# State scan of a four-part network: softplus in one activation, convolution sums in SBUF, earlier norm statistics

## The reference, cut to what matters

```python
xz = x @ in_proj_w + in_proj_b
xc, z = jnp.split(xz, 2, axis=-1)
xc = silu(depthwise_causal_conv4(xc) + conv_b)
dBu = xc @ x_proj_w + x_proj_b
delta_s, B, u = jnp.split(dBu, [d_state, 2 * d_state], axis=-1)
delta = jax.nn.softplus(delta_s @ dt_proj_w + dt_proj_b)
A = -jnp.arange(1, d_state + 1)
deltaA = jnp.exp(delta[..., None] * A)
deltaB_u = delta[..., None] * B[:, :, None, :] * u[..., None]
h = dA * h + dBu_      # over time, y = h.sum(-1)
y = (y + u * D) * jax.nn.silu(z)
return y @ out_proj_w + out_proj_b
```

## Time and profile before

| | us |
|---|---|
| median of 3 runs (1362.57 to 1373.91) | 1366.16 |
| the profiled execution | 1378.29 |
| its span in the trace | 1376.6 |
| PE / DVE / ACT / POOL busy in the span | 1197.3 / 904.7 / 782.9 / 291.6 |
| scan: first scan instruction to the end of the last | 1017.40 to 1228.10 |

### The profile page before, as it was taken

The page is one execution under the profiler, slowest core; times in us unless marked ns, Lnnn a source line. Parts: engine busy times, 40 slices in busy tenths (PEclk is TensorE's granted clock), DMA queues, the critical chain, the costliest instruction groups (busy, mean ns, idle before and its releaser), DMA issues.

```text
span 1376.6 us, 15993 instructions
## 1 busy us (share of the span) xinstructions
PE 1197.3 (87%) x5776; PEld 603.1 (44%) x5776; DVE 904.7 (66%) x1684; ACT 782.9 (57%) x1135; POOL 291.6 (21%) x208
## 2 busy tenths in 40 slices
PE   4669886788999999999999999999968879779998
PEld 2345453343433333333333365655533334237776
DVE  4566866688788788887863264344467978984443
ACT  3667752354544565555678844545768677525554
POOL 3223344210000000000000110100056968750000
PEclk9779878899999999999999999999989899899999
DMA  2222157524300000000000121221131312200000
GB/s 91 62 62 63 47 100 114 102 31 90 43 1 1 1 1 1 2 1 1 1 2 24 58 72 32 91 64 36 40 107 63 116 69 108 88 12 0 8 8 16
DMA packets 52111, 62.98 MB, mean 46 GB/s; under 512 B 7864, under 2 KB 42304, under 8 KB 49984
## 3 DMA queue, kind: packets, MB, share of 16 engines
q1 hardware_dynamic: 52032, 61.95, 17.3%
HBM read 51.05 MB, written 4.46 MB: 40 GB/s over the span
## 4 chain that ended last, share of the span: by engine, by line
PE 54%; DVE 18%; ACT 10%; POOL 6%; issue 4%; DMA 1%; SPq 1%; DVEq 0%; POOLq 0%; ACTq 0%
DVE mx L1142 9%; PE psum L1230 8%; PE psum L1513 7%; PE psum L1200 6%; PE psum L1130 6%; PE psum L388 5%; PE psum L390 5%; PE psum L389 5%; PE psum L1905 4%; POOL drive L1954 3%; ACT probs L1214 2%; DVE hst L1972 1%; ACT psum L1914 1%; DMA kz<-qk_part_rows 1%; PE psum L1203 1%
## 5 line engine op out<-in xcount | busy, mean ns | idle before, releaser
L1214 ACT ACTIVATE probs<-psum 128x1024 f32<-128x1024 f32 (+1 forms) x320 | 288.4, 938 | 207.2 <-PE psum L1200 106.5
L1142 DVE TENSOR_REDUCE mx<-psum 128x1 f32<-128x512 f32 (+3 forms) x640 | 345.6, 602 | 67.0 <-PE psum L1130 50.4
L1130 PE MATMUL psum<-kz,qa 128*128 128x512 bf16 (+3 forms) x640 | 194.2, 356 | 39.3 <-DVE mx L1142 22.9
L1200 PE MATMUL psum<-qa,kz 128*128 128x512 bf16 (+1 forms) x640 | 186.0, 365 | 5.1 <-ACT probs L1214 2.8
L1905 PE MATMUL psum<-hst,ident 128*128 128x512 f32 x256 | 133.7, 669 | 34.7 <-DVE hst L1972 18.0
L1954 POOL TENSOR_TENSOR drive<-du,b_bc 128x1024 f32<-128x1024 f32 x64 | 149.3, 2354 | 11.7 <-DVE hst L1972 11.0
L1230 PE MATMUL psum<-probs,v 128*32 128x512 f32 (+3 forms) x1280 | 150.6, 543 | 0.1
L1531 DVE TENSOR_TENSOR hid<-hid,gate_bc 128x1024 f32<-128x1024 f32 x64 | 78.8, 1242 | 109.0 <-ACT hid L1523 106.9
L1523 ACT ACTIVATE hid<-psum,cols 128x512 f32<-128x512 f32 x128 | 85.0, 689 | 76.2 <-PE psum L390 75.7
L1972 DVE TENSOR_TENSOR_SCAN hst<-psum,hlast,drive 128x512 f32<-128x512 f32 x96 | 115.5, 1262 | 15.6 <-ACT psum L1914 10.0
L1130 PEld LDWEIGHTS psum<-kz,qa 128*128 128x128 bf16 x640 | 61.2, 99 | 142.0 <-DVE mx L1142 85.3
(11 more groups left out here) (293 smaller groups left out, 1844.0 us busy)
## 6 DMA issues: line engine op xcount, KB each, us to landing
b_bc<-b_rows SPq DMA_DIRECT2D x16, 1024.0 KB, 4.7
cs_bc<-cs_rows SPq DMA_DIRECT2D x16, 512.0 KB, 6.2
gate_bc<-gate_rows SPq DMA_DIRECT2D x32, 256.0 KB, 3.2
ew_raw<-experts_dram SPq DMA_DIRECT2D x8, 512.0 KB, 3.5
qk_part_rows<-qk_parts SPq DMA_DIRECT2D x8, 384.0 KB, 2.7
qa<-qk_part_rows SPq DMA_DIRECT2D x48, 64.0 KB
kz<-qk_part_rows SPq DMA_DIRECT2D x96, 32.0 KB
fw_raw<-net_dram SPq DMA_DIRECT2D x11, 256.0 KB, 2.7
```

The costliest lines, as they stand in the source:

```text
L1130: ins = pe.matmul(out[:, 0:w], qa[:, b, h // 2, i * P:(i + 1) * P], kz[:, h // 8, c, h % 8, 0:w], start=True, stop=not last, skip_group_ch ...
L1142: dve.tensor_reduce(mx[:, 4 * i + h % 4, c:c + 1], fill_bank("mx", k, n)[:, 0:w], AX.X, ALU.max).then_inc(S["mx_read"], 1)
L1200: ins = pe.matmul(out[:, lo:], kz[:, h // 8, kt // TPB, h % 8, kt % TPB * P:(kt % TPB + 1) * P], qa[:, b, h // 2, lo:], start=True, stop=n ...
L1214: act.activation(probs[:, st % 2, hh, :, lo:], s_pair[n % 2][:, :, lo:], ACT.Exp, scale=SCALE).then_inc(S["p_done"], 1)
```

## The change

Softplus is one activation function from PSUM straight into delta; dv1, da1, abs, ln and the VectorE instruction for delta go. The convolution's tap and its sums are in xc (SBUF) instead of in "cv" banks, and silu works in place. z's product stands behind state 3 on TensorE and its silu directly behind the silu of xc, after state 6. dt's activation stands behind state 10, u behind 11, du behind 12. The norm statistics stand behind state 7 (not 13), GpSimd's part of the norm behind drive 13 (not 12), counted (-2). DRIVE_SLOTS goes from 3 to 5. The waits for delta_ready ahead of state 0 on ScalarE become waits for c_dt_read.

```diff
-DRIVE_SLOTS = 3
+DRIVE_SLOTS = 5
...
-        MF_PE = {22: ("turn",), 25: ("x",), 28: ("db",), 29: ("dt", "z"), 30: ("u",)}
-        MF_ACT = {22: ("apply",), 23: ("hi",), 25: ("x", "tap"), 27: ("xc",), 28: ("db",), 29: ("dt", "z"),
-                  30: ("abs", "ln", "u")}
-        MF_DVE = {21: ("stats",), 26: ("conv0",), 27: ("conv1",), 31: ("delta", "du")}
+        MF_PE = {22: ("turn",), 25: ("x",), 26: ("z",), 28: ("db",), 29: ("dt",), 30: ("u",)}
+        MF_ACT = {22: ("apply",), 23: ("hi",), 25: ("x", "tap"), 27: ("xc", "z"), 28: ("db",),
+                  29: ("dt",), 30: ("u",)}
+        MF_DVE = {21: ("stats",), 26: ("conv0",), 27: ("conv1",), 31: ("du",)}
...
-        FRONT_DVE = [(-3, "stats"), (3, "conv0"), (4, "conv1"), (12, "delta"), (13, "du")]
-        FRONT_POOL = [(-3, "ln")]
+        FRONT_DVE = [(-9, "stats"), (3, "conv0"), (4, "conv1"), (12, "du")]
+        FRONT_POOL = [(-2, "ln")]
...
             elif part == "tap":
+                if b >= 1:
+                    act.wait_ge(S["c_u_filled"], 2 * b)
                 for j in range(2):
                     act.wait_ge(S["c_in_read"], 4 * b + j + 1)
-                    n = scan_index("cv", b, j)
-                    if n is not None:
-                        act.wait_ge(*n)
-                    act.activation(scan_bank("cv", b, j)[:, :], cin1[:, j, 0:BLK], ACT.Identity,
+                    act.activation(xc[:, j, :], cin1[:, j, 0:BLK], ACT.Identity,
                                    scale=C("conv1_w", CONV * j)).then_inc(S["c_tap"], 1)
...
-                    act.activation(xc[:, j, :], scan_bank("cv", b, j)[:, :], ACT.Silu, bias=C("conv1_b", j)).then_inc(S["xc_ready"], 1)
+                    act.activation(xc[:, j, :], xc[:, j, :], ACT.Silu, bias=C("conv1_b", j)).then_inc(S["xc_ready"], 1)
...
-            elif part == "dt":
+            else:
+                if b >= 2:
+                    act.wait_ge(S["decay_done"], NS1 * (b - 1))
+                    act.wait_ge(S["delta_ready"], 2 * (b - 1))
                 for m in range(2):
                     act.wait_ge(S["c_dt_filled"], 2 * b + m + 1)
-                    act.activation(dv1[:, m, :], scan_bank("dt", b, m)[:, :], ACT.Identity,
+                    act.activation(delta[:, b % 2, m, :], scan_bank("dt", b, m)[:, :], ACT.Softplus,
                                    bias=C("dt1_b", m)).then_inc(S["c_dt_read"], 1)
-            elif part == "abs":
-                act.wait_ge(S["c_dt_read"], 2 * b + 2)
-                o.did(act.activation(da1[:, :, :], dv1[:, :, :], ACT.Abs))
-                o.wait()
-                abs_done[b] = o.did(act.activation(da1[:, :, :], da1[:, :, :], ACT.Exp, scale=-1.0))
-            else:
-                act.wait_ge(S["act_order"], abs_done[b])
-                act.activation(da1[:, :, :], da1[:, :, :], ACT.Ln, bias=one[:, 0:1]).then_inc(S["dt_lnd"], 1)
...
-                        acc = scan_bank("cv", b, j)[:, :]
+                        acc = xc[:, j, :]
...
-                o.did(dve.scalar_tensor_tensor(delta[:, b % 2, :, :], dv1[:, :, :], 0.0, da1[:, :, :], ALU.max, ALU.add))
```

More of the change, by code:

```diff
@@ L308, in build @@
         dB = sb("dB", [P, BLK], F32)
-        dv1 = sb("dv1", [P, 2, BLK], F32)
-        da1 = sb("da1", [P, 2, BLK], F32)
         delta = sb("delta", [P, 2, 2, BLK], F32)
@@ L1696, in build @@
         LN_C = 3 * NB
-        FRONT_PE = [(0, "turn"), (1, "x"), (7, "db"), (9, "dt"), (11, "z"), (13, "u")]
-        FRONT_ACT = [(-1, "apply"), (0, "hi"), (2, "x"), (2, "tap"), (6, "xc"), (7, "db"), (9, "dt"), (10, "abs"),
-                     (11, "z"), (12, "ln"), (13, "u")]
-        FRONT_DVE = [(-3, "stats"), (3, "conv0"), (4, "conv1"), (12, "delta"), (13, "du")]
-        FRONT_POOL = [(-3, "ln")]
-        RING_FRONT = [(0, "turn"), (1, "x"), (2, "tap"), (7, "db"), (9, "dt"), (11, "z"), (13, "u")]
-        EARLIEST = -3
+        FRONT_PE = [(0, "turn"), (1, "x"), (3, "z"), (7, "db"), (9, "dt"), (11, "u")]
+        FRONT_ACT = [(-1, "apply"), (0, "hi"), (2, "x"), (2, "tap"), (6, "xc"), (6, "z"), (7, "db"), (10, "dt"), (11, "u")]
+        FRONT_DVE = [(-9, "stats"), (3, "conv0"), (4, "conv1"), (12, "du")]
+        FRONT_POOL = [(-2, "ln")]
+        RING_FRONT = [(0, "turn"), (1, "x"), (3, "z"), (7, "db"), (9, "dt"), (11, "u")]
+        EARLIEST = -9
         POST_Y, POST_PE, POST_DVE, POST_POOL = 3, 7, 6, 8
@@ L1721, in part_names @@
             return {"turn": [("x", b, 0)], "x": [("in", b, 0), ("in", b, 1)], "z": [("in", b, 2), ("in", b, 3)],
-                    "tap": [("cv", b, 0), ("cv", b, 1)], "u": [("u", b, 0), ("u", b, 1)], "db": [("db", b, 0)],
+                    "u": [("u", b, 0), ("u", b, 1)], "db": [("db", b, 0)],
                     "dt": [("dt", b, 0), ("dt", b, 1)]}[part]
@@ L1726, in scan_emptied @@
             return {"x": (S["xT_hi"], NB + b + 1), "in": (S["c_in_read"], 4 * b + j + 1), "u": (S["delta_ready"], 2 * b + j + 1),
-                    "cv": (S["xc_ready"], 2 * b + j + 1),
                     "db": (S["c_db_read"], b + 1), "dt": (S["c_dt_read"], 2 * b + j + 1),
@@ L1743, in scan_bank @@
             return (scan_fill0 if b == 0 and kind != "out" else scan_fill1).bank(kind, b, j)
[L1745 to L1749, removed]
         def scan_take(pe, kind, b, j):
@@ L1825, in scan_front_act @@
                     act.wait_ge(S["conv_done"], 2 * NB + 2 * b + j + 1)
-                    if b >= 1:
-                        act.wait_ge(S["c_u_filled"], 2 * b)
-                    act.activation(xc[:, j, :], scan_bank("cv", b, j)[:, :], ACT.Silu, bias=C("conv1_b", j)).then_inc(S["xc_ready"], 1)
+                    act.activation(xc[:, j, :], xc[:, j, :], ACT.Silu, bias=C("conv1_b", j)).then_inc(S["xc_ready"], 1)
             elif part == "u":
@@ L1886, in scan_front_dve @@
                             ins.then_inc(S["conv_done"], 1)
-            elif part == "delta":
-                dve.wait_ge(S["dt_lnd"], NB + b + 1)
+            else:
                 if b >= 2:
-                    dve.wait_ge(S["decay_done"], NS1 * (b - 1))
                     dve.wait_ge(S["drive_done"], NS1 * (b - 1))
-                o.did(dve.scalar_tensor_tensor(delta[:, b % 2, :, :], dv1[:, :, :], 0.0, da1[:, :, :], ALU.max, ALU.add))
-            else:
-                o.wait()
+                dve.wait_ge(S["c_dt_read"], 2 * b + 2)
                 for m in range(2):
@@ L1910, in state_act @@
             if n == 0:
-                act.wait_ge(S["delta_ready"], 2 * b + 2)
+                act.wait_ge(S["c_dt_read"], 2 * b + 2)
             if k >= 2:
```

1 line of the change is left out of this document (removed).

## The result

| | before | after |
|---|---|---|
| median of 19 runs, us | 1369.13 (1362.57 to 1378.57) | 1380.42 (1369.84 to 1384.8) |
| ratio of the runs, after to before | | 1.006 [1.004, 1.008] |
| span of the profiled execution, us | 1376.6 | 1371.3 |
| scan stage: first scan to the end of the last, us | 210.6 | 218.5 |

The changed kernel is 0.6% slower: by the ratio 8.2 us, by its interval 5.5 to 11. (The two medians lie further apart, 11.3 us; the runs of each kernel spread over some 15 us, so the interval is the safer guide.) The two spans point the other way. They are single executions, and the one of after had already gained 12.3 us ahead of the experts, in code that the change leaves alone (the norm ahead of them on VectorE starts at 709.78 us, before at 722.04). So what follows compares lengths inside the scan, which grew by 7.9 us.

What follows compares the result with a forecast made beforehand. The prediction took VectorE to bound the scan, busy 185.1 of 210.7 us. Savings of 20.4 us and 24.4 us added gave +4.0 us, from a median of 1366.2 to 1370.2 us, range 1350 to 1382.

Steps and rivals of the forecast that it cites:

- slower by over 1%: Whole kernel: the outcome of a time above 1379.8 us, given a chance of 0.14.
- (1): Ends of scan blocks 0 and 1: GpSimd no longer stops for norm statistics, so four VectorE gaps go, 7.1 us saved.
- (2): Scan, VectorE: the delta instruction goes because Softplus writes delta itself, 5.8 us saved.
- (3): Scan, ScalarE: silu visits joined, one Softplus visit; 13.0 us of decay waits fall to 6.0, saving 7.0.
- (4): MoE tail at unit 30: ScalarE loses some 7 us of work, but only the last down product gains, 0.5 us.
- Convolution: Scan, VectorE: accumulations with sums in SBUF take turns with GpSimd's drives, adding 24.4 us, bounds 9.4 to 42.
- The sign: What would show the forecast right in the convolution: accumulations of some 2.9 us in a mean, in turns with drives.
- The walk: Step-by-step count of convolution turns: 7.6 us in block 0, 2.35 for its conv1, 7.2 each in blocks 1 and 2.
- the statistics come after state 7: Scan: norm statistics move ahead so that GpSimd no longer stops; no cost was priced for the move.
- A: Convolution: VectorE keeps the pair, one drive delays each of four parts, 9.4 us; net -11.0, 1355 us; chance 0.20.
- B: Convolution: accumulations meet no drive or read without cost from the pair; net -20.4, 1346 us; chance 0.08.
- C: Convolution: GpSimd has a drive ready at all 18 accumulations, 42.3 us; net +21.9, 1388 us; chance 0.10.

Runs made afterwards that it cites:

- e7: The kernel before with only the norm part: statistics behind state 7, GpSimd's norm behind drive 13, three drive slots; 1363.3 us, ratio to before 0.9937.
- e8: The kernel before with only Softplus from PSUM into delta behind state 9, the rest as before; 1357.8 us, ratio to before 0.9901.
- e2: The changed kernel with the convolution's sums back in PSUM and z's product behind state 11; 1353.6 us, ratio to before 0.9876.
- e1: The kernel before with only the convolution part: tap and sums in xc (SBUF), three drive slots; 1386.3 us, ratio to before 1.011.
- e6: The changed kernel with GpSimd's drive of state 6 held until that block's convolution is done; 1366.6 us, ratio to before 0.9954.
- e3: The changed kernel with three drive slots instead of five; 1368.5 us, ratio to before 0.9996.
- e4: The changed kernel with the two small tensor_scalar of the norm on GpSimd instead of VectorE; 1375.7 us, ratio to before 1.0043.
- e5: The changed kernel with the convolution's sums back in PSUM and the two small norm instructions on GpSimd; 1354.8 us, ratio to before 0.987.

## Why the prediction was right in its verdict, and what it missed

I forecast a change within 1% (+4.0 us), by turns between accumulations and drives, and within 1% it came: +7.2 us by the stages (7.9 in the scan, 0.6 given back ahead of it) and 8.2 by the ratio. It is nearly twice the forecast, and 19 runs do tell it from none. The forecast in absolute time, 1370.2 us, was 10 us low, partly because it stood on a median of three runs, 3 us below that of 19: the median of after, 1380.42, is inside the range with 1.6 us to spare, and above the 1379.8 that I had drawn for "slower by over 1%". By its own steps:

- **(1) Norm stops, 7.1 us:** right. All four gaps are gone in after, and e7 takes them away alone.
- **(2) Delta, 5.8 us:** right, 5.84 us in the rows. e7 adds that it would have cost 10 us had it stayed behind the earlier statistics.
- **(3) ScalarE's visits, 7.0 us saved, 6.0 left:** 6.1 us are left. A visit of 3.83 us was worked out and 3.83 measured; the gap of 1.4 us was 1.68 once and 1.44 twice, with 0.88 behind it in block 2 alone where I had 0.6 in each. Behind the joint visit of the two silus I find no more than one gap of 0.23 us, in block 2. But the saving isn't where I had put it. Softplus alone leaves 13.6 of 14.5 us of these waits (e8); the earlier norm alone, which I had booked only under (1), leaves 8.8 (e7), and in e2, without the joint visit, 8.3 are left. A total that comes out right from terms that overlap is partly luck.
- **(4) MoE tail, 0.5 us:** about 0.6: the start of the scan moved 12.9 us between the two traces (1017.40 to 1004.49), 12.3 of which lay ahead of the experts. From the first activation of the experts to the first scan instruction the trace before shows 229.12 us, after 228.50, and those of e1 and e7, which leave this part alone, 229.11 and 229.12. The last down product on TensorE in after, against the earlier trace rows, shows 0.35 us of it:

```profile
988.06 7.03 PE L1511 MATMUL psum<-hid,ew_raw 128*128 128x512 f32 x16
```

- **Convolution, 24.4 us:** 23.05. The walk gave 7.6 + 2.35 + 7.2 + 7.2; the rows give 9.80 - 2.70 = 7.1, then 3.48 - 1.39 = 2.1, and 6.9 twice, with conv1 free in blocks 1 and 2 as said. The difference is the length of a turn: a drive and an accumulation took 2.8 us together, not the 2.9 to 2.95 that I counted, and in block 0 conv1 lost 2.1, not 2.35. (The sign that I gave, a mean of 2.9 us an accumulation, didn't agree with my own sum, which makes 2.1 for the 18; it was 2.0, with the clean ones among them.) The cause, turns with GpSimd, is shown from three sides: e2 takes away the second SBUF operand, e6 takes away GpSimd, and e3 takes away its turns.
- **The step that failed in size: "the statistics come after state 7", costed at nothing.** I had looked at who waits for them and not at what runs beside them. Behind state 13 GpSimd had stood idle waiting for them, so the two small tensor_scalar met nobody (0.17 us each). Behind state 7 drives run without a pause. They took 6.16 us, not 0.68: +5.5 us. e7 has the cost without any other part of the change (+3.1), e2 without the convolution (+4.3), and e4 takes it away.

What is left is small: shorter scans and the overlap of neighbouring instructions, 0.8 us less together, waits for x_tok 0.9 longer, and 0.8 less of other waits. From +4.0 one comes to 4.0 + 5.5 - 1.35 - 0.8 + 0.9 - 0.8, about +7.4, against the 7.2 of the stages. That the missed 5.5 us did not lead out of the range is luck: they were as large as the whole forecast, and the walk's excess of 1.35 us paid for a quarter of them.

The Trainium skill (SBUF — State Buffer, Who interferes with whom), whose rule on two SBUF inputs I had used, names the missed case in the same list: tensor_scalar can run in a mode that takes both port pairs, and then the later of the two engines waits for the whole instruction of the other. The trace agrees in the waits (0.17 us alone, up to 2.28 beside drives), though it doesn't name the mode, and also on what the page exempts: bn_stats and bn_aggr, with one input, come to the same 2.4 us in the scan of both kernels, and the accumulations in PSUM keep their 0.74.

**The rivals.** A (VectorE keeps the pair, one drive for each part of the convolution) falls: four accumulations met four turns, not one. B (no cost) falls with the same row. C (a drive ready at all 18) falls because the five slots and the bias step did stop GpSimd before conv1 in blocks 1 and 2: 1.38 us.

**Where the gain of the three parts went.** Alone, they change the scan by +11.9 (e1), -6.3 (e7) and -9.1 us (e8), -3.5 together; the whole change gives +7.9. Busy and idle time of VectorE split the 11.4 us between. Busy time sums to 5.0 us less in the three than in the whole (+17.5 + 6.0 - 6.7 against +21.9). By kind of instruction: the accumulations are 4.4 us longer in the whole than in e1 and the small instructions 2.3 longer than in e7, both of which have three slots (e3 takes 5.8 and 2.1 us off the whole by going to three); against that e7 lengthens delta by 4.2 us, which the whole no longer has; the rest, some 2.5 us, is spread over the scans and the overlap of neighbouring instructions, and its cause stays open. The idle time sums to 6.3 us more gain than the whole has (-20.3 against -14.0). I read this as longer instructions and freed engines filling the same gaps, each of which can be filled only once; no run separates it.

**Left open:** why TensorE's dt product is late in block 1 of e5, and whether a better place for it would turn e5's 3.0 us of new gaps into time. It wasn't tried, and it stays open why the part ahead of the scan is 1.4 us longer in e4 and e5. Nor was e2 run with three slots: whether five help once the sums are in PSUM is not shown. Of after's 2.8 us for a turn, less than the sum of the two clean lengths, I only know the size.

The best version that was run is e2 (or e5, the same within its interval): Softplus, early statistics and five slots, the sums left in PSUM; 1.2% faster than before and, by the two ratios (0.9876 / 1.006), 1.8% faster than after.

## What to carry to other kernels

Before an accumulation moves from PSUM to SBUF, or a small instruction moves anywhere, look at what GpSimd does at that time: here the same instruction took 0.72 or 2.8 us, and a 128x4 one 0.17 or 2.28. More buffers for the engine off the path can make the path slower, since they let it take turns that it was kept from (10.4 us here between three slots and five, with the sums in SBUF). And one stall can shelter another instruction: where you take a stall away, price again what ran in its shade (delta, 1.22 to 3.3 us).

## What the runs showed of the hardware that I had not expected

- A vector instruction with two SBUF inputs and GpSimd's tensor_tensor alternate one for one while both queues are full: each shows 2.8 us where the drive alone is 2.33 and the accumulation 0.72. So GpSimd loses too.
- A tensor_scalar of 128x4, from SBUF to SBUF, waits for a whole drive: up to 2.28 us for 0.17 us of work. The drives beside it keep their 2.35 us. It is 13 times its own length, where an accumulation grows to four times.
- Softplus as an activation function: 688 ns for 128x512 from PSUM, with a load of 1283 ns on either side and no pause between load and activation (1042.50 + 1.28, next at 1043.80).
